# Main matmuls of a two-layer kernel as pairs of 64-row halves, low-rank part spread over the steps

## The chip, the cores and the metric

One core of one Trainium2 chip runs one launch. The metric is the device time in microseconds. TensorE multiplies, VectorE (DVE) and ScalarE (ACT) copy, subtract and activate, GpSimd (POOL) and SyncE (SP) mostly start transfers.

## The reference

The input x is 32 sequences of 64 tokens with 1024 features, in fp32. Two layers:

```
h  = cond(x): 64 x 64 matrix of the sequence's condition, over the tokens
x  = x + W3 (silu(W1 h + b1) * (W2 h + b2)) + b3           1024 x 1024 each
y  = W x + B[i] (A[i] x)            i: adapter of the sequence, rank 16
c  = softmax(keys . (Wq mean(y)) / sqrt(128))               8 experts
x  = x + W_org y + sum_e c_e up_e (down_e y)                rank 64 each
```

## The kernel before

Features lie on the partitions, tokens along the free dimension. The tokens are worked in two halves of 1024, each in six stages: `up0`, `up1` (the two halves of W1 and W2 with the gate), `down` (W3), `lin` (W with the adapters), `exp` (W_org and the experts' down matrix), `expup` (the experts' up matrix).

A stage other than `expup` computes its 2 x 2 block product with 7 block products instead of 8 (Strassen's scheme in the form with reused sums; the page calls them by i = 0 to 6). `S1` to `S4` are sums of input blocks, `T1` to `T4` sums of weight blocks, all made by VectorE (lines 927 to 938 and 979). `expup` has 4 plain products. The list `PRODUCTS` has 78 entries (stage, i).

A product has 4 groups of 128 output rows (`exp` has 6: the last two are the experts' down matrix), each group in its own PSUM bank of 512 columns. Every operand is split in a high and a low part of type fp32r: ScalarE casts `s_hi` and `t_hi` (lines 809, 828), VectorE subtracts for `s_lo` and `t_lo` (line 897). A group is 4 row blocks `p` of 128 times 3 terms: hi x hi (line 634), hi x lo (635), lo x hi (636), 12 matmuls of 128 rows, 128 output columns and 512 tokens. The main matmuls are 340 x 12 = 4080. `s` has two buffers, `t` has four slots of two groups (a half).

When a group is done it counts in `group_done`, and a half (two groups) is taken from its banks by one operation on 1024 columns: `snap` (ScalarE copy, line 840), `add` (VectorE, line 995), `addb` with bias (per group, line 1005), `gate` (per group, line 1027), `eadd` (line 1015) or `esnap` (line 843). Products i = 0, 2, 3, 4 use banks 0 to 3, the others banks 4 to 7, groups 4 and 5 of `exp` a table. `wait_bank_free` holds TensorE until the former content of a bank is taken.

Each engine's program runs in order, written out by hand in a loop over the products n. VectorE in loop n: the takings left from n - 1, `s_lo` of n + 1, `t_lo` of n + 1, gates, S sums, T sums, taking of half 0 of n. ScalarE: `s_hi` of n + 1, snaps left from n - 1, `t_hi` of n + 1, silus, first snap of n.

The low-rank part of `lin` (`lora_out`) is added in products 1, 4, 5 and 6: `xr` holds A x masked so that rows 0 to 63 serve tokens 0 to 255 and rows 64 to 127 the others. It runs as one lump after group 1: 4 turns of 2 fp32 matmuls of 64 rows and 256 columns (each two records in the profile), the two on different row halves of the array and different banks; turns 2 and 3 wait for turns 0 and 1 (`lora_crossed`), since two row halves may not write one bank at once. `route` puts the router's small matmuls (lines 743, 749, 757) after group 5 of `exp` 3 and group 1 of `exp` 4 and 5. `mixing` (line 731) makes the conditional product at the start of each half; `lora_in` (line 713) makes A x in `lin` 0 and 1.

Of the kernel before, what the change touches and what calls it, by code (L numbers as in the profile page):

```python
# [12 lines left out]
P = 128  # L13
# [4 lines left out]
TN = 512  # L18
# [82 lines left out]

def s_new(n):
    return S_LAST.index(S_LAST[S_ID[n]]) == S_ID[n] and not (kind_of(n) == "expup" and PRODUCTS[n][1] >= 2)


def t_halves(n, when):
# [100 lines left out]

GROUP_AT, SNAP_AT, SUM_AT, TMADE_AT, LOAD_AT = {}, {}, {}, {}, {}  # L210
for _n in range(LAST + 1):
    for _g in range(groups_in(_n)):
        GROUP_AT[_n, _g] = len(GROUP_AT) + 1
    _acts = (act_snaps(_n - 1) + act_silus(_n - 1) if _n else []) + act_first(_n)
    for _what in _acts:
        SNAP_AT[_what] = len(SNAP_AT) + 1
    _dves = (dve_after(_n - 1) + dve_post(_n - 1) if _n else []) + dve_own(_n)[0] + dve_own(_n)[1] + dve_scales(_n)
    for _what in _dves:
        SUM_AT[_what] = len(SUM_AT) + 1
    for _what in t_sums_beside(_n):  # L220
        TMADE_AT[_what] = len(TMADE_AT) + 1
# [23 lines left out]
def t_at(n, j):  # L245
    return T_ID[n, j] + 1
# [10 lines left out]
def build(nc, x_pairs, x_t, idx, cond_t, b_upgate, b_down, lora_a, lora_b, keys_t, wq_t,  # L257
# [3 lines left out]
    with ExitStack() as ctx:  # L261
# [62 lines left out]
        a_laid = sem("a_laid")  # L324
        b_diffed = sem("b_diffed")
        xr_full, xr_ready = sem("xr_full"), sem("xr_ready")
        lora_crossed = sem("lora_crossed")
        y_summed = sem("y_summed")
        q_full, q_copied = sem("q_full"), sem("q_copied")
        scores_full = sem("scores_full")  # L330
# [294 lines left out]
                    store(h, u, 1)  # L625

        def tensor_engine(pe):
            def product(n, g, p, start, stop):
                out = banks[:, bank_of(n, g), :]
                at, slot = (g % 2 * 4 + p) * P, T_ID[n, g // 2] % 4  # L630
                w_hi, w_lo = t_hi[:, slot, at:at + P], t_lo[:, slot, at:at + P]
                slot = S_ID[n] % 2
                x_hi, x_lo = s_hi[:, slot, p * TN:(p + 1) * TN], s_lo[:, slot, p * TN:(p + 1) * TN]
                pe.matmul(out, w_hi, x_hi, start=start, stop=False, skip_group_check=True)  # L634
                pe.matmul(out, w_hi, x_lo, start=False, stop=False, skip_group_check=True)  # L635
                return pe.matmul(out, w_lo, x_hi, start=False, stop=stop, skip_group_check=True)  # L636

            def wait_bank_free(n, g):

# [39 lines left out]
                else:  # L679
                    wait_taken(pe, n - {2: 2, 3: 1, 4: 1, 5: 4, 6: 1}[i], g)  # L680

            def lora_out(n):

                s, i = PRODUCTS[n]
                t = 1 if i >= 5 else 0
                crossed = 2 * (4 * STAGES[s][0] + (1, 4, 5, 6).index(i))
                for turn in range(4):
                    if turn >= 2:  # L690
                        pe.wait_ge(lora_crossed, crossed + turn - 1)
                    for j in range(2):
                        g, rows = 2 * (turn % 2) + (turn // 2 + j) % 2, slice(64 * j, 64 * (j + 1))
                        col = (g if i in (1, 6) else 4 + g) * P
                        last = pe.matmul(banks[:, bank_of(n, g), j * 2 * P:(j + 1) * 2 * P],  # L695
                                         lora_b_sb[rows, t, col:col + P], xr[rows, t, :],
                                         start=turn == 1 and i in (1, 5), stop=False, skip_group_check=True)
                    if turn < 2:
                        last.then_inc(lora_crossed, 1)
                    if turn == 2:  # L700
                        last.then_inc(group_done, 2)

            def lora_in(h, t, bank):
                s = stage_of(h, "lin")
# [26 lines left out]
                        last = pe.matmul(out[:, k, :], x_c[:, k * P:(k + 1) * P], mix[:, c, :], start=True, stop=True)  # L731
                    last.then_inc(mixed_full, 1)

            def route(n, g):

                s, i = PRODUCTS[n]
                h = STAGES[s][0]
                if (i, g) == (3, 5):
# [7 lines left out]
                if (i, g) == (4, 1):  # L746
# [4 lines left out]
                if (i, g) == (5, 1):  # L751
                    wait_taken(pe, n - 1, 3)
                    pe.wait_ge(rows_done, h + 1)
                    pe.wait_ge(consts_made, 5)
                    for k in range(KE):
                        rows = coef_rows[:, 2 * k:2 * k + 2, :].rearrange("b e r -> b (e r)")
                        last = pe.matmul(coef_bank[:, k * BH:(k + 1) * BH], rows, ident[:, :],
                                         start=True, stop=True)
                    last.then_inc(coef_full, 1)

            pe.wait_ge(mix_zeroed, 2)
            for n in range(LAST + 1):
                s, i = PRODUCTS[n]
# [6 lines left out]
                for g in range(groups_in(n)):  # L770
                    pe.wait_ge(s_ready, S_ID[n] + 1)
                    pe.wait_ge(t_ready, t_at(n, g // 2))
                    wait_bank_free(n, g)
                    fresh = g >= 4 or kind == "expup" or i in (0, 1, 5)
                    begun = lora and g >= 2
                    for p in range(4):
                        last = product(n, g, p, fresh and p == 0 and not begun, p == 3)
                    if lora and g == 1:
                        pe.wait_ge(xr_ready, h * TILES + (2 if i >= 5 else 1))
                        pe.wait_ge(b_gathered, (h + 1) * BH * 16)  # L780
                        if i == 6:
                            pe.wait_ge(b_diffed, h + 1)
                        wait_bank_free(n, 2)
                        wait_bank_free(n, 3)
                        lora_out(n)
                    elif not lora or g >= 2:
                        last.then_inc(group_done, 1)
                    if kind == "exp":
                        route(n, g)

        def scalar_engine(act):
            for j in range(2):
# [77 lines left out]
            for n in range(LAST + 1):  # L870
                s, i = PRODUCTS[n]
                h, kind = STAGES[s]
                if n < LAST and kind_of(n + 1) != "up0" or i < 6 and kind == "up0":
                    s_split(n + 1)
                if n > 0:
                    take(act_snaps(n - 1))
                if n < LAST:
                    t_split(n + 1, 0)
                if n > 0:
                    take(act_silus(n - 1))  # L880
                if kind == "down" and i in (2, 3):
                    lay_a(h, i - 2)
                take(act_first(n))
                if n < LAST:
                    t_split(n + 1, 1)
                if kind == "exp" and i == 4:
                    act.wait_ge(bias_done, h + 1)
                    act.activation(sexp[:, :], router[0:BH, 32:32 + E], ACT.Exp, bias=sbias[:, :],
                                   scale=SCORE_SCALE, accum_out=ssum[:, :]).then_inc(exp_done, 1)
                if n < LAST:  # L890
                    t_split(n + 1, 2)
                if kind == "expup" and i == 3 and h + 1 < HALVES:
                    mixing(h + 1)

        def vector_engine(dve):
# [186 lines left out]
            for n in range(LAST + 1):  # L1082
# [9 lines left out]
                    s_split(n + 1)  # L1092
                if n < LAST:
                    t_split(n + 1, 0)
                if kind == "lin" and i == 1:
                    mask_xr(h, 1, 7)
                if n > 0:
# [12 lines left out]
                if kind == "exp" and i == 4:  # L1110
                    largest(h)
                if kind == "exp" and i == 5:
                    copy_coef(h)
                if n < LAST:
                    t_split(n + 1, 1)
                if kind == "exp":
# [2 lines left out]
                take(dve_own(n)[1])  # L1119
                if kind == "exp" and i == 4:  # L1120
                    soften(h)
                take(dve_scales(n))
                if n < LAST:
                    t_split(n + 1, 2)
# [69 lines left out]
```

## Time and profile before

| | us |
|---|---|
| median of 3 runs | 1012.61 (1011.53 to 1012.75) |
| the profiled execution | 1012.33 |
| its span, first to last instruction | 1010.5 |
| TensorE busy | 990.6, 4772 matmul records |
| VectorE busy | 743.0 |
| ScalarE busy | 391.3 |
| mean granted TensorE clock | 0.998 |

PE is TensorE's matmuls, PEld its weight loads; the two overlap, and so do the records of successive matmuls. The distance from start to start tells what a matmul costs, its duration does not.

### The profile page before, as it was taken

To read this page: it belongs to the slowest core of one execution; us is meant where nothing else is said; L and a number is where in the kernel's file an instruction comes from. 1 tells how busy PE (TensorE), PEld (TensorE's weight loads), DVE (VectorE), ACT (ScalarE), POOL (GpSimd) and SP (SyncE) were. 2 spreads that over 40 slices of the span, in tenths; PEclk is the share of its full clock that TensorE was granted. 3 is DMA by queue.
4 is the path that set the end of the run, shared out by engine and by line. 5 is a ranking of instruction groups with operands and counts; after the bars stand their busy time and mean duration, and the time that the engine had idled before them with its cause. 6 is when DMAs were issued, how large, how long until landed. Compare 5 with 4: busy or idle time off the path is not lost.

```text
span 1010.5 us, 12337 instructions
## 1 busy us (share of the span) xinstructions
PE 990.6 (98%) x4772; PEld 820.0 (81%) x4772; DVE 743.0 (74%) x574; ACT 391.3 (39%) x349; POOL 33.8 (3%) x55
## 2 busy tenths in 40 slices
PE   6999999999999999999999999999999999999997
PEld 6888888878787888888888888888778878888886
DVE  2877977997866889674437888789885859877641
ACT  6563553543344333331055544543342532423110
POOL 1500000000000000000100000000000000000011
PEclk9999999999999999999999999999999999999999
DMA  8122044034013001322331211521330230021012
GB/s 279 76 84 104 1 157 175 23 112 159 1 42 131 36 1 63 149 100 89 121 126 42 83 42 40 210 84 32 121 140 2 75 134 0 1 105 42 1 63 104
DMA packets 22985, 84.68 MB, mean 84 GB/s; under 512 B 2690, under 2 KB 6802, under 8 KB 17042
## 3 DMA queue, kind: packets, MB, share of 16 engines
q1 hardware_dynamic: 20370, 74.98, 20.6%
q0 software_dynamic: 2400, 8.41, 2.2%
q8 instruction: 39, 0.64, 0.3%
q10 hardware_dynamic: 160, 0.52, 0.2%
q14 instruction: 16, 0.13, 0.0%
HBM read 75.51 MB, written 8.39 MB: 83 GB/s over the span
## 4 chain that ended last, share of the span: by engine, by line
PE 95%; DVE 2%; DMA 1%; issue 1%; ACT 0%; POOL 0%; POOLq 0%; ACTq 0%
PE banks L634 30%; PE banks L635 30%; PE banks L636 30%; PE banks L731 3%; PE banks L695 2%; PE banks L713 1%; DMA st<-x_pairs_in 1%; DMA cond_sb<-cond_t_in 1%; DVE st L938 0%; DVE w L979 0%; DVE s_lo L897 0%; ACT s_hi L809 0%; DVE r L995 0%; PE banks L743 0%; DVE t_lo L897 0%
## 5 line engine op out<-in xcount | busy, mean ns | idle before, releaser
L634 PE MATMUL banks<-s_hi,t_hi 128*128 128x512 f32 x1360 | 531.7, 391 | 2.8 <-DVE r L995 2.8
L635 PE MATMUL banks<-s_lo,t_hi 128*128 128x512 f32 x1360 | 529.4, 389 | 0.0
L636 PE MATMUL banks<-s_hi,t_lo 128*128 128x512 f32 x1360 | 529.2, 389 | 0.0
L634 PEld LDWEIGHTS banks<-s_hi,t_hi 128*128 128x128 f32 x1360 | 255.2, 188 | 60.0 <-issue 7.2
L636 PEld LDWEIGHTS banks<-s_hi,t_lo 128*128 128x128 f32 x1360 | 255.3, 188 | 53.3
L635 PEld LDWEIGHTS banks<-s_lo,t_hi 128*128 128x128 f32 x1360 | 255.3, 188 | 52.3
L995 DVE TENSOR_TENSOR r<-banks,r 128x1024 f32<-128x1024 f32 x92 | 111.4, 1221 | 100.3 <-PE banks L636 95.7
L897 DVE TENSOR_TENSOR t_lo<-w,t_hi 128x1024 fp32r<-128x1024 f32 x132 | 156.6, 1220 | 3.2 <-ACT t_hi L828 3.2
L809 ACT CAST s_hi<-st 128x2048 fp32r<-128x2048 f32 x40 | 76.5, 1912 | 197.7 <-PE banks L636 145.0
L828 ACT CAST t_hi<-w 128x1024 fp32r<-128x1024 f32 x132 | 133.3, 1048 | 50.4 <-PE banks L636 50.4
L809 ACT CAST s_hi<-r 128x2048 fp32r<-128x2048 f32 x34 | 65.0, 1913 | 206.7 <-PE banks L636 181.7
L897 DVE TENSOR_TENSOR s_lo<-st,s_hi 128x2048 fp32r<-128x2048 f32 x40 | 91.7, 2292 | 51.4 <-ACT s_hi L809 51.3
L897 DVE TENSOR_TENSOR s_lo<-r,s_hi 128x2048 fp32r<-128x2048 f32 x34 | 77.9, 2290 | 57.0 <-ACT s_hi L809 57.0
L979 DVE TENSOR_TENSOR w<-w 128x1024 f32<-128x1024 f32 x48 | 57.3, 1221 | 0.0
L828 ACT CAST t_hi<-we 128x1024 fp32r<-128x1024 f32 x30 | 30.9, 1052 | 60.0 <-PE banks L636 52.5
L840 ACT COPY r<-banks 128x1024 f32<-128x1024 f32 x40 | 40.4, 1010 | 24.4 <-PE banks L636 20.0
L731 PE MATMUL banks<-mix,st 128*128 128x128 f32 x256 | 32.3, 292 | 8.9 <-POOL mix L450 7.9
L731 PEld LDWEIGHTS banks<-mix,st 128*128 128x128 f32 x256 | 31.8, 207 | 9.2 <-issue 9.2
L1015 DVE TENSOR_TENSOR r<-banks,r 128x1024 f32<-128x1024 f32 x14 | 17.0, 1223 | 28.8 <-PE banks L636 28.8
L897 DVE TENSOR_TENSOR t_lo<-we,t_hi 128x1024 fp32r<-128x1024 f32 x30 | 36.0, 1221 | 0.0
L617 POOL DMA_DIRECT2D out_t<-r x16 | 11.6, 727 | 522.0 <-DVE r L995 522.0
L1005 DVE SCALAR_TENSOR_TENSOR r<-banks,b_dn_sb,r 128x512 f32<-128x512 f32 x32 | 22.3, 747 | 7.6 <-PE banks L636 7.6
(59 smaller groups left out, 329.9 us busy)
## 6 DMA issues: line engine op xcount, KB each, us to landing
w<-w_up_in SPq DMA_DIRECT2D x16, 1024.0 KB, 4.8
w<-w_base_in SPq DMA_DIRECT2D x10, 1024.0 KB, 4.8
st<-x_pairs_in SPq DMA_DIRECT2D x16, 512.0 KB, 5.7
w<-w_down_in SPq DMA_DIRECT2D x8, 1024.0 KB, 5.3
r<-x_t_in SPq DMA_DIRECT2D x8, 1024.0 KB, 6.2
w<-w_lin_in SPq DMA_DIRECT2D x8, 1024.0 KB, 5.2
out_t<-r POOLq DMA_DIRECT2D x16, 512.0 KB, 3.2
we<-w_expin_in SPq DMA_DIRECT2D x10, 512.0 KB, 4.5
```

The costliest lines, as they stand in the source:

```text
L634: pe.matmul(out, w_hi, x_hi, start=start, stop=False, skip_group_check=True)
L635: pe.matmul(out, w_hi, x_lo, start=False, stop=False, skip_group_check=True)
L636: return pe.matmul(out, w_lo, x_hi, start=False, stop=stop, skip_group_check=True)
L695: last = pe.matmul(banks[:, bank_of(n, g), j * 2 * P:(j + 1) * 2 * P], lora_b_sb[rows, t, col:col + P], xr[rows, t, :], start=turn == 1 an ...
L731: last = pe.matmul(out[:, k, :], x_c[:, k * P:(k + 1) * P], mix[:, c, :], start=True, stop=True)
L809: act.copy(s_hi[:, S_ID[n] % 2, :], s_source(n)).then_inc(s_hi_done, 1)
L828: act.copy(t_hi[:, T_ID[n, j] % 4, :], t_source(n, j)).then_inc(t_hi_done, 1)
L840: act.copy(half_block(n, at), half_banks(n, at)).then_inc(snapped, 1)
L897: return dve.tensor_tensor(out, value, hi.bitcast(F32), ALU.subtract)
L979: dve.tensor_tensor(out, left, right, ALU.subtract).then_inc(t_made, 1)
L995: dve.tensor_tensor(half_block(n, at), half_banks(n, at), half_block(n, at), ALU.add).then_inc(summed, 1)
L1005: dve.scalar_tensor_tensor(out=group_block(n, at), in0=banks[:, bank_of(n, at), :], scalar=b_dn_sb[:, m:m + 1], in1=group_block(n, at), op ...
```

## The change

Every product runs in steps (pair of groups, back). In a step with back = 0 each main matmul becomes two of 64 rows: rows 0 to 63 into the bank of the pair's first group, rows 64 to 127 into that of the second; with back = 1 the rows are exchanged. So a step is 4 x 3 x 2 = 24 matmuls. The order of steps is in `steps`. The second step of a pair waits for `crossed` of the first. Both groups are counted done together, at the end of the second step. The low-rank part is two matmuls at the end of each of the four steps. `route` follows other places: step (2, 1) of `exp` 3, (0, 0) of `exp` 4, (1, 1) of `exp` 5. On ScalarE the snaps left over go ahead of `s_hi`, and the exponential ahead of `t_hi` of the second half; on VectorE `largest` goes ahead and `copy_coef` behind. Both functions `half_rows` and `lora_half` replace `product` and `lora_out`.

```diff
+def steps(n):
+    if groups_in(n) == 4:
+        return [(0, 0), (1, 0), (0, 1), (1, 1)]
+    if PRODUCTS[n][1] == 1:
+        return [(0, 0), (1, 0), (0, 1), (1, 1), (2, 0), (2, 1)]
+    return [(0, 0), (1, 0), (0, 1), (2, 0), (1, 1), (2, 1)]
...
-            def product(n, g, p, start, stop):
-                out = banks[:, bank_of(n, g), :]
-                at, slot = (g % 2 * 4 + p) * P, T_ID[n, g // 2] % 4
-                w_hi, w_lo = t_hi[:, slot, at:at + P], t_lo[:, slot, at:at + P]
-                slot = S_ID[n] % 2
-                x_hi, x_lo = s_hi[:, slot, p * TN:(p + 1) * TN], s_lo[:, slot, p * TN:(p + 1) * TN]
-                pe.matmul(out, w_hi, x_hi, start=start, stop=False, skip_group_check=True)
-                pe.matmul(out, w_hi, x_lo, start=False, stop=False, skip_group_check=True)
-                return pe.matmul(out, w_lo, x_hi, start=False, stop=stop, skip_group_check=True)
+            def half_rows(n, g, p, j, term, start):
+                rows, at = slice(64 * j, 64 * (j + 1)), (g % 2 * 4 + p) * P
+                weights = (t_hi, t_hi, t_lo)[term][rows, T_ID[n, g // 2] % 4, at:at + P]
+                acts = (s_hi, s_lo, s_hi)[term][rows, S_ID[n] % 2, p * TN:(p + 1) * TN]
+                return pe.matmul(banks[:, bank_of(n, g), :], weights, acts, start=start, stop=False,
+                                 skip_group_check=True)
...
+            def lora_half(n, g, j):
+                i, rows = PRODUCTS[n][1], slice(64 * j, 64 * (j + 1))
                 t = 1 if i >= 5 else 0
...
+                col = (g if i in (1, 6) else 4 + g) * P
+                return pe.matmul(banks[:, bank_of(n, g), j * 2 * P:(j + 1) * 2 * P], lora_b_sb[rows, t, col:col + P],
+                                 xr[rows, t, :], start=False, stop=False, skip_group_check=True)
...
+                for pair, back in steps(n):
+                    if back:
+                        pe.wait_ge(crossed, CROSSED_AT[n, pair])
+                    else:
+                        pe.wait_ge(s_ready, S_ID[n] + 1)
+                        pe.wait_ge(t_ready, t_at(n, pair))
+                        for g in groups_of(pair):
+                            wait_bank_free(n, g)
                     for p in range(4):
-                        last = product(n, g, p, fresh and p == 0 and not begun, p == 3)
-                    if lora and g == 1:
+                        for term in range(3):
+                            for j in range(2):
+                                last = half_rows(n, 2 * pair + (back + j) % 2, p, j, term, (fresh or pair == 2)
+                                                 and not back and p == 0 and term == 0)
+                    if lora:
                         pe.wait_ge(xr_ready, h * TILES + (2 if i >= 5 else 1))
...
+                        for j in range(2):
+                            last = lora_half(n, 2 * pair + (back + j) % 2, j)
+                    if back:
+                        last.then_inc(group_done, 2)
+                    else:
+                        last.then_inc(crossed, 1)
                     if kind == "exp":
-                        route(n, g)
+                        route(n, pair, back)
...
@@ scalar_engine
+                if n > 0:
+                    take(act_snaps(n - 1))
                 if n < LAST and kind_of(n + 1) != "up0" or i < 6 and kind == "up0":
                     s_split(n + 1)
-                if n > 0:
-                    take(act_snaps(n - 1))
```

## Rows read from the trace of the kernel before

**Rows 1.** The page: busy time by engine, granted clock by slice, chain that ended last.

```profile
PE 990.6 (98%) x4772; PEld 820.0 (81%) x4772; DVE 743.0 (74%) x574; ACT 391.3 (39%) x349; POOL 33.8 (3%) x55
...
PEclk9999999999999999999999999999999999999999
...
PE banks L634 30%; PE banks L635 30%; PE banks L636 30%; PE banks L731 3%; PE banks L695 2%; PE banks L713 1%; DMA st<-x_pairs_in 1%; DMA cond_sb<-cond_t_in 1%; DVE st L938 0%; DVE w L979 0%; DVE s_lo L897 0%; ACT s_hi L809 0%; DVE r L995 0%; PE banks L743 0%; DVE t_lo L897 0%
```

**Rows 2.** Groups by shape: count, busy us, mean ns, idle before.

```profile
L634 PE MATMUL banks<-s_hi,t_hi 128*128 128x512 f32 x1360 | 531.7, 391 | 2.8 <-DVE r L995 2.8
...
L634 PEld LDWEIGHTS banks<-s_hi,t_hi 128*128 128x128 f32 x1360 | 255.2, 188 | 60.0 <-issue 7.2
...
L695 PEld LDWEIGHTS banks<-xr,r 64*128 64x128 f32 x128 | 11.6, 185 | 4.0 <-issue 2.8
```

**Rows 3.** Busy time in stretches (length; PE, PEld, DVE, ACT, POOL): up1, down, lin.

```profile
101.35:177.50 76.15, 76.15 (x337) 63.06 (x336) 62.27 (x48) 37.26 (x35) 0.00 (x0) 1.00 0.29 111
177.50:255.40 77.90, 76.48 (x337) 62.80 (x335) 69.85 (x58) 31.03 (x27) 1.29 (x1) 1.00 0.28 95
258.76:345.93 87.17, 87.17 (x468) 70.28 (x465) 61.61 (x42) 32.21 (x28) 0.00 (x0) 1.00 0.17 61
```

**Rows 4.** Timeline (start us, duration us, engine) around the first low-rank lump.

```profile
277.09 0.39 PE L636 MATMUL banks<-s_hi,t_lo 128*128 128x512 f32 x1
277.41 1.60 PEld L695 LDWEIGHTS banks<-xr,r 64*128 64x128 f32 x16 [0.35 <-issue]
277.41 2.00 PE L695 MATMUL banks<-xr,r 64*128 64x256 f32 x16
...
279.34 0.50 PE L634 MATMUL banks<-s_hi,t_hi 128*128 128x512 f32 x1
...
279.68 0.40 PE L635 MATMUL banks<-s_lo,t_hi 128*128 128x512 f32 x1
...
279.92 0.40 PE L636 MATMUL banks<-s_hi,t_lo 128*128 128x512 f32 x1
```

**Rows 5.** TensorE of line 695 in short stretches (x: records touched by the stretch).

```profile
277.72:277.94 0.22, 0.22 (x4) 1.00 0.00 0
...
278.38:278.59 0.21, 0.21 (x4) 1.00 0.00 0
```

**Rows 6.** Full-row fp32: mixing in one stretch, then the router's matmuls in the timeline.

```profile
18.00:25.05 7.05, 7.05 (x65) 7.05 (x64) 1.00 0.93 309
...
411.21 1.85 PE L743 MATMUL banks<-y_sum,cond_sb 128*128 128x16 f32 x16
412.92 0.49 PE L634 MATMUL banks<-s_hi,t_hi 128*128 128x512 f32 x1
```

**Rows 7.** Timeline of VectorE in down, products 2 and 3.

```profile
208.37 1.22 DVE L995 TENSOR_TENSOR r<-banks,r 128x1024 f32<-128x1024 f32 x1
210.35 1.23 DVE L995 TENSOR_TENSOR r<-banks,r 128x1024 f32<-128x1024 f32 x1 [0.76 <-PE banks L636]
212.30 2.29 DVE L897 TENSOR_TENSOR s_lo<-st,s_hi 128x2048 fp32r<-128x2048 f32 x1 [0.72 <-ACT s_hi L809]
214.51 2.35 DVE L897 TENSOR_TENSOR t_lo<-w,t_hi 128x1024 fp32r<-128x1024 f32 x2
216.78 2.29 DVE L938 TENSOR_TENSOR st<-r 128x2048 f32<-128x2048 f32 x1
218.98 2.35 DVE L979 TENSOR_TENSOR w<-w 128x1024 f32<-128x1024 f32 x2
221.25 2.35 DVE L995 TENSOR_TENSOR r<-banks,r 128x1024 f32<-128x1024 f32 x2
```

**Rows 8.** Waits of TensorE: us in total, times, longest.

```profile
PE banks L634 <- DVE r L995: 2.8, 2, 1.4
```

**Rows 9.** Timeline at the end of down: VectorE, then TensorE.

```profile
256.03 2.72 DVE L1005 SCALAR_TENSOR_TENSOR r<-banks,b_dn_sb,r 128x512 f32<-128x512 f32 x4
...
256.88 1.95 PE L713 MATMUL banks<-r 128*32 128x128 f32 x64 [1.33 <-issue]
```

More of the change, by code:

```diff
@@ L206, in dve_scales @@
     return [("scale", n, 0), ("scale", n, 1)] if kind_of(n) == "exp" and PRODUCTS[n][1] == 5 else []
-GROUP_AT, SNAP_AT, SUM_AT, TMADE_AT, LOAD_AT = {}, {}, {}, {}, {}
+GROUP_AT, CROSSED_AT, SNAP_AT, SUM_AT, TMADE_AT, LOAD_AT = {}, {}, {}, {}, {}, {}
 for _n in range(LAST + 1):
+    for _pair, _back in steps(_n):
+        if not _back:
+            CROSSED_AT[_n, _pair] = len(CROSSED_AT) + 1
     for _g in range(groups_in(_n)):
@@ L326, in build @@
         xr_full, xr_ready = sem("xr_full"), sem("xr_ready")
-        lora_crossed = sem("lora_crossed")
+        crossed = sem("crossed")
         y_summed = sem("y_summed")
@@ L680, in wait_bank_free @@
                     wait_taken(pe, n - {2: 2, 3: 1, 4: 1, 5: 4, 6: 1}[i], g)
-            def lora_out(n):
-                s, i = PRODUCTS[n]
+            def lora_half(n, g, j):
+                i, rows = PRODUCTS[n][1], slice(64 * j, 64 * (j + 1))
                 t = 1 if i >= 5 else 0
[L688 to L701, printed above, removed]
+                col = (g if i in (1, 6) else 4 + g) * P
+                return pe.matmul(banks[:, bank_of(n, g), j * 2 * P:(j + 1) * 2 * P], lora_b_sb[rows, t, col:col + P],
+                                 xr[rows, t, :], start=False, stop=False, skip_group_check=True)
             def lora_in(h, t, bank):
@@ L732, in mixing, with route @@
                     last.then_inc(mixed_full, 1)
-            def route(n, g):
+            def route(n, pair, back):
                 s, i = PRODUCTS[n]
                 h = STAGES[s][0]
-                if (i, g) == (3, 5):
+                if (i, pair, back) == (3, 2, 1):
                     pe.wait_ge(wq_loaded, 16)
@@ L745, in route @@
                     last.then_inc(q_full, 1)
-                if (i, g) == (4, 1):
+                if (i, pair, back) == (4, 0, 0):
                     pe.wait_ge(q_copied, h + 1)
@@ L750, in route @@
                               start=True, stop=True).then_inc(scores_full, 1)
-                if (i, g) == (5, 1):
+                if (i, pair, back) == (5, 1, 1):
                     wait_taken(pe, n - 1, 3)
@@ L769, in tensor_engine @@
                 lora = kind == "lin" and i in (1, 4, 5, 6)
[L770 to L775, printed above, removed]
-                    for p in range(4):
-                        last = product(n, g, p, fresh and p == 0 and not begun, p == 3)
-                    if lora and g == 1:
+                fresh = kind == "expup" or i in (0, 1, 5)
+                for pair, back in steps(n):
[6 more added lines that the diff above has]
+                            wait_bank_free(n, g)
+                    for p in range(4):
+                        for term in range(3):
[3 more added lines that the diff above has]
+                    if lora:
                         pe.wait_ge(xr_ready, h * TILES + (2 if i >= 5 else 1))
@@ L782, in tensor_engine @@
                             pe.wait_ge(b_diffed, h + 1)
[L783 to L787, printed above, removed]
+                        for j in range(2):
[4 more added lines that the diff above has]
+                        last.then_inc(crossed, 1)
                     if kind == "exp":
-                        route(n, g)
+                        route(n, pair, back)
         def scalar_engine(act):
@@ L883, in scalar_engine @@
                 take(act_first(n))
-                if n < LAST:
-                    t_split(n + 1, 1)
                 if kind == "exp" and i == 4:
@@ L889, in scalar_engine @@
                                    scale=SCORE_SCALE, accum_out=ssum[:, :]).then_inc(exp_done, 1)
+                if n < LAST:
+                    t_split(n + 1, 1)
                 if n < LAST:
@@ L1094, in vector_engine @@
                     t_split(n + 1, 0)
+                if kind == "exp" and i == 4:
+                    largest(h)
                 if kind == "lin" and i == 1:
@@ L1109, in vector_engine @@
                 take(dve_own(n)[0])
[L1110 to L1113, printed above, removed]
                 if n < LAST:
@@ L1121, in vector_engine @@
                     soften(h)
+                if kind == "exp" and i == 5:
+                    copy_coef(h)
                 take(dve_scales(n))
```

## The prediction, made before any run of the changed kernel

> **What bounds the kernel now.** I read the page first. TensorE is busy for 990.6 of 1010.5 us, its clock is granted in full in nearly every slice, and nine tenths of the chain that ended last lie on the three lines of the main matmul [rows 1]. So what counts is how far apart two main matmuls start, and where TensorE waits. The grouped instructions give the number of them: 3 x 1360 = 4080, each with its own weight load of 188 ns that lies beside a stream [rows 2]. The table by stretches then gives their distance: in one stage without any wait, 7 products of 48 matmuls take 76.15 us, so 0.2266 us each; the next stage takes 77.90 us up to its last product's end, 1.6 us more [rows 3]. A stream of 512 columns at the granted 2.4 GHz lasts 512/2.4 = 213.3 ns. Each matmul therefore carries 13.3 ns in which nothing streams: 4080 x 13.3 = 54 us in the whole kernel. That gap is the only large thing that this change can touch, because it takes no column out.
>
> **What a pair costs (the term that decides).** After the change a step is 12 pairs: two 512-column streams side by side, on rows 0-63 and 64-127, on two banks, each with its own 128-column weight load. A product of four groups is 4 steps, so 48 pairs, in the place of 48 matmuls. The trace of before has no pair of this kind. Its nearest row is the low-rank part at line 695: 16 records in 2.00 us, 64 x 256, in full fp32 [rows 4]. Cut into windows of 0.21 to 0.22 us, every window touches four of them, two that began in it and two that end in it [rows 5]. So two do run side by side, and the next two follow 0.216 us later. A record there is 256 columns at two cycles, as long a stream as the main one (213.3 ns), and the gap is 2.7 ns instead of 13.3. If the main pairs behave so, one costs 0.2160, and the gain is 4080 x (0.2267 - 0.2160) = 43.7 us.
>
> The row does not prove it. It differs from the main matmul in two things: 64 rows instead of 128, and fp32 at two cycles a column instead of one. The mixing matmuls are full-row fp32: 65 records within 7.05 us, of which two or three began before the window, so about 0.112 us for 128 columns x 2 cycles = 0.107 us [rows 6]. Full rows alone do not bring a gap of 13 ns, then; that speaks for the data rate or for the weight load read beside a full-rate stream as its cause, which halving the rows need not cure. So the bounds are: 0.2160 at best (line 695), 0.2267 if the gap stays, and 2 x 13.3 ns on 213.3 = 0.2400 if the gap is a price for each load. I take 0.2160, since line 695 is nearest in rows, in load and in length of stream, but only at a little over one half.
>
> The Trainium skill ("TensorE: Matmul & The Clock Gate", section "Wait — 56ns, not 53.3ns?") has 215.7 ns between back-to-back matmuls of 512 columns, that is 2.5 ns over the stream. The trace disagrees for the present form (226.6) and agrees for the line 695 pairs (216); by that figure the sum would be the one above.
>
> **The low-rank part.** Now it is four turns of two matmuls in one lump. From the last full matmul before it, 277.09, to the second one behind it, 279.68, lie 2.59 us where two distances would be 0.45; then a few distances of 0.24 follow before the old rhythm returns [rows 4]: 2.19 us in all. Of these 8 x 0.216 = 1.73 is streaming, some 0.20 lies on either side where the engine goes from 128 to 64 rows and back, and 0.06 is the slow rhythm. Spread over the four steps, the streaming stays and the changes of form go: 8 x 0.46 = 3.7 us gained.
>
> **New changes of form.** The router's matmuls of 128 rows stand now between full-row matmuls: 16 records from 411.21 in 1.85 us, and the next main one starts at 412.92, as soon as their loads allow [rows 6]. After the change both sides are a change of form, 0.2 each by rows 4. With mixing to first product the same. The column-form and 16-row matmuls (lines 713, 749, 757) pay it already. Bounds: 0 and 6 x 0.4 = 2.4 us; I take 1.5.
>
> **The new waits.** Each second step waits for `crossed` of the first step of the same pair of banks. In 76 of 78 products another step of 2.59 us lies between, and inside line 695 the same kind of wait costs nothing (the 0.216 goes on through it). In product 1 of each `exp` stage steps (2,0) and (2,1) are adjacent: the end of the last matmul (0.39 us after its start), the signal and the way in cost about 0.4, twice: 0.8 us. Behind this wait stands everything on TensorE, and nobody else.
>
> **What comes later or is needed earlier.** Groups 0 and 1 are now finished after 3/4 of a product instead of 1/4 and 1/2; t of the second half and the second pair of banks are needed after 1/4 instead of 1/2. So the cover for taking a bank out shrinks from 5.4 to 2.6 us (products 3, 4 and 6 reuse the banks of the product before). The cost of taking is 1.23 us on VectorE or 1.0 on ScalarE; what matters is the queue ahead. On ScalarE the snaps now go ahead of the 1.9 us s_hi; on VectorE the `largest` of the router goes earlier, because its result is now needed at step 4 of `exp` 4; both fit by about 2 us. Where VectorE has room (`up1` and `lin`: 62.27 of 76.15 and 61.61 of 87.17 us [rows 3]; `up0` and `expup` are like `up1` or emptier) the add of the first half starts at 3/4 + 0.2 us and ends 1.2 us before the next product. There I lose about 0.3 us per half, at product 2 of the `up` stages, whose t_lo would be ready 0.1 to 0.2 late.
>
> `down` is the place where VectorE is full: 69.85 of 77.90 us [rows 3], one operation on another, with two gaps of 0.7 us around 210 only [rows 7]. Worked with those durations (add 1.14 apart, s_lo 2.20, t_lo 1.14, S 2.20, T 1.14), with the start of `down` 0 as zero: add(down 2, half 0) ends at 32.6, about where product 3 begins now (3 x 10.88 = 32.64), but TensorE would be there at 31.4. Product 3 then starts at the old time and three products gain nothing. The wait ahead of product 4 (1.4 us of TensorE, twice [rows 8]) is for add(3, half 0), behind S3 and two T sums [rows 7]. Its queue starts 1 us sooner, because the product before no longer ends last: product 4 gains 1.1, products 5 and 6 0.5 each together with it. At the end of the stage TensorE already waits 1.3 us for the bias add behind four T sums, which hangs on the same s_hi [rows 9]; there nothing is gained. `down` gives 2.3 of 3.6 us a half: 1.3 x 2 = 2.6 lost, and 0.6 for the `up` stages. For waits that I have not found, 0 to 8, I take 2.
>
> **The instruction stream.** 4080 more matmuls and loads. In the low-rank lump 32 records pass in 2.00 us, 62 ns each with the streams as their bound; a main pair has 4 in 216 ns, 54 each. Loads and DMA bytes of data are unchanged. Cost nought while TensorE's queue is full.
>
> **Sum.** The profiled execution took 1012.33 us around a span of 1010.5; the median of three is 1012.61, 0.03% above. 1012.33 - 43.7 - 3.7 + 1.5 + 0.8 + 2.6 + 0.6 + 2 = 972.4 us.
>
> **The rivals.**
> - *The gap stays* (0.2267 a pair). For it: the full-row fp32 rows without a gap [rows 6], which leave the full-rate stream as the cause. Then only the low-rank gain remains, -3.7 + 1.5 + 0.8, and since products are no shorter the `down` queue is as now, with 0 to 2 of new waits: 1011 to 1014, say 1012.
> - *The two loads are served one after the other.* The 128-row loads of line 743 follow each other every 0.112 us (16 in 1.71 us, with 16-column streams [rows 6]); two would be 0.223, more than the stream. Gain 4080 x 0.0034 = 13.9: about 998. Against it: at line 695 all 16 loads and 16 streams pass at 0.216 a pair, though loads there could also hide by luck. The Trainium skill (the same page, "LDWEIGHTS (loading the stationary operand)") says that load time goes by columns and not by rows, so halving the rows would double the load work; that speaks against the change, and a 64-row load lasts 185 ns and a 128-row load 188 [rows 2], so the trace agrees on one load and leaves open whether two go side by side at the full rate.
> - *Slower: the gap is paid once for each load.* Two tiles each load while both stream, so a pair is 213.3 + 2 x 13.3 = 0.240: 4080 x 0.0133 = 54 us more, about 1066. It decides from a pair of 0.2270 upwards. Against it: at line 695 the pair has less gap than the single matmul.
> - *The pairs don't run side by side at full rate.* 0.43 a pair, some 1880 us. Line 695 runs them at half the data rate only, so it is not excluded; nearly.
>
> **How the numbers follow.** Chances: pairs at 0.216 0.52 (own range 963 to 990, with waits from 0 to 8 and a pair from 0.2150 to 0.2190); loads in turn 0.07; gap stays 0.22, of which within 0.2% 0.17, faster 0.02, slower 0.03; gap per load 0.14; anything worse 0.05. About 0.2% (2 us) is what a measurement of this kernel can tell. Faster 0.52 + 0.07 + 0.02 = 0.61, same 0.17, slower 0.14 + 0.03 + 0.05 = 0.22. The range reaches from the low end of the first case over the second and third: 962 to 1016, which holds 0.81.
>
> **What would show it.** Main matmuls in twos a few ns apart, the next two 0.216 later; `up1` in about 72.7 us instead of 76.15; plain products of 10.4 and `exp` products of 15.6 us; low-rank products about 12.1; a wait for VectorE's line 995 ahead of product 3 of `down` too. A pair at 0.227 or 0.240 makes the prediction wrong whatever else holds; a pair at 0.216 with more than 8 us of new TensorE waits says that the cover of the banks was the misjudged part.

## The result and the profile after

| | before | after |
|---|---|---|
| median, us | 1012.68 (4 runs, 1011.53 to 1013.48) | 1024.65 (4 runs, 1023.01 to 1027.08) |
| ratio to before | | 1.0121 (95%: 1.0097 to 1.0145) |
| profiled execution, us | 1012.33 | 1023.86 |

The changed kernel is slower by 12 us. The forecast was 972.4, so the direction was wrong, and the time lies outside the range of 962 to 1016.

The page of the kernel after, with the lines that answer to [rows 1, 2], and the instruction queue (packets, MB; before it had 39 and 0.64):

```profile
PE 994.1 (97%) x8852; PEld 857.7 (84%) x8852; DVE 744.0 (73%) x574; ACT 392.4 (38%) x349; POOL 33.9 (3%) x55
...
q8 instruction: 71, 1.16, 0.5%
...
L646 PE MATMUL banks<-s_hi,t_hi 64*128 64x512 f32 x2720 | 552.1, 393 | 8.3 <-DVE xr L1048 5.3
...
L646 PEld LDWEIGHTS banks<-s_hi,t_hi 64*128 64x128 f32 x2720 | 268.8, 185 | 54.5 <-issue 10.8
```

Every main matmul has become two (2720 for 1360 on one of three terms), as the diff says, and before them stands a releaser that was not there: VectorE's mask of the low-rank part, 5.3 us. The stretches that answer to [rows 3], `up1`, `down` and `lin` of the first half:

```profile
103.56:179.72 76.16, 76.16 (x676) 62.94 (x673) 62.27 (x48) 37.48 (x35) 0.00 (x0) 1.00 0.30 111
179.72:257.60 77.88, 76.34 (x674) 68.35 (x672) 69.78 (x58) 31.04 (x27) 1.29 (x1) 1.00 0.28 96
261.34:351.63 90.29, 87.62 (x802) 83.46 (x800) 61.16 (x42) 32.21 (x28) 0.00 (x0) 0.98 0.17 59
```

Read the first line against 76.15 us before: 7 x 48 = 336 pairs take 76.16 us, 0.2267 each, to four digits what one full-row matmul cost. `down` is as before too (77.88 against 77.90). `lin` took 87.17 in the stretch of [rows 3] and takes 90.29 here. The timeline of TensorE in `up0` (start, duration, x: records) shows the pairs, two records together and the next two 0.22 to 0.23 us later:

```profile
60.03 0.39 PE L646 MATMUL banks<-s_hi,t_lo 64*128 64x512 f32 x2
60.26 0.39 PE L646 MATMUL banks<-s_hi,t_hi 64*128 64x512 f32 x2
60.49 0.39 PE L646 MATMUL banks<-s_lo,t_hi 64*128 64x512 f32 x2
```

The halves do run side by side at the full rate, then; what did not come is the shorter gap. And in `lin` product 1 stands the only large wait that was not there before (the first line; the second is the wait of [rows 8]):

```profile
PE banks L646 <- DVE xr L1048: 5.3, 2, 2.7
PE banks L646 <- DVE r L1001: 2.8, 2, 1.5
```

```profile
275.40 2.29 DVE L903 TENSOR_TENSOR s_lo<-st,s_hi 128x2048 fp32r<-128x2048 f32 x1 [4.38 <-ACT s_hi L815]
...
277.18 0.59 PE L699 MATMUL banks<-xr,r 64*128 64x256 f32 x4
277.62 2.35 DVE L903 TENSOR_TENSOR t_lo<-we,t_hi 128x1024 fp32r<-128x1024 f32 x2
279.88 0.42 DVE L1048 TENSOR_TENSOR xr<-banks,half_mask 128x256 f32<-128x256 f32 x1
...
280.45 0.50 PE L646 MATMUL banks<-s_hi,t_hi 64*128 64x512 f32 x2 [2.67 <-DVE xr L1048]
...
281.22 0.69 PE L646 MATMUL banks<-s_hi,t_hi 64*128 64x512 f32 x2
...
281.64 0.69 PE L646 MATMUL banks<-s_lo,t_hi 64*128 64x512 f32 x2
...
282.07 0.69 PE L646 MATMUL banks<-s_hi,t_lo 64*128 64x512 f32 x2
```

The first fence is TensorE's waits (us in total, times, longest), the second the timeline. The second low-rank input lies in bank 7 until VectorE masks it out (`mask_xr`, line 1048), and group 3 of `lin` 1 writes to bank 7. Before, group 3 began at three quarters of the product. Now the pair of groups 2 and 3 is the second step and begins at one quarter. VectorE still makes `s_lo` and two `t_lo` first, so TensorE stands for 2.67 us. A little behind the wait the pairs start 0.42 to 0.43 us apart instead of 0.227. The granted clock (the last three columns are the clock, DMA share and GB/s), below for the idle time and two stretches behind it,

```profile
277.40:280.40 3.00, 0.38 (x4) 0.00 (x0) 2.90 (x4) 0.00 (x0) 0.00 (x0) 1.00 0.00 0
280.40:281.21 0.81, 0.76 (x6) 0.76 (x8) 0.00 (x0) 0.00 (x0) 0.00 (x0) 1.00 0.00 0
281.21:284.62 3.41, 3.41 (x18) 3.14 (x16) 0.00 (x0) 0.00 (x0) 0.00 (x0) 0.50 0.00 0
```

is still full for 0.8 us when the matmuls go on, then half, the level of 1.2 GHz, for 3.41 us. The eight pairs or so at that level cost 8 x 0.2 = 1.6 us more. So `lin` 1 lasts 17.17 us, start to start, against 13.20 before, in both halves.

### The profile page after: what moved, and what is told of

It is laid out like the page before. It is cut to its first block, busy times and chain, and to the rows that moved or that the text cites. A ratio compares the mean times of both kernels' runs of the same rounds, so it can differ in the third digit from the quotient of the medians.

```text
span 1022.1 us, 20505 instructions
## 1 busy us (share of the span) xinstructions
PE 994.1 (97%) x8852; PEld 857.7 (84%) x8852; DVE 744.0 (73%) x574; ACT 392.4 (38%) x349; POOL 33.9 (3%) x55
## 3 DMA queue, kind: packets, MB, share of 16 engines
q8 instruction: 71, 1.16, 0.5%
## 4 chain that ended last, share of the span: by engine, by line
PE 93%; DVE 3%; DMA 2%; issue 1%; ACT 1%; POOL 0%; POOLq 0%; ACTq 0%; DVEq 0%
PE banks L646 88%; PE banks L730 2%; DMA st<-x_pairs_in 1%; PE banks L699 1%; DVE t_lo L903 1%; DVE s_lo L903 1%; ACT s_hi L815 1%; DMA cond_sb<-cond_t_in 1%; DVE w L985 0%; PE banks L712 0%; PE banks L742 0%; DVE st L944 0%; DVE r L1001 0%; PE banks L756 0%; POOLq L1134 0%
## 5 line engine op out<-in xcount | busy, mean ns | idle before, releaser
L646 PE MATMUL banks<-s_hi,t_hi 64*128 64x512 f32 x2720 | 552.1, 393 | 8.3 <-DVE xr L1048 5.3
L646 PE MATMUL banks<-s_hi,t_lo 64*128 64x512 f32 x2720 | 545.0, 387 | 0.0
L646 PE MATMUL banks<-s_lo,t_hi 64*128 64x512 f32 x2720 | 544.8, 387 | 0.0
L646 PEld LDWEIGHTS banks<-s_hi,t_hi 64*128 64x128 f32 x2720 | 268.8, 185 | 54.5 <-issue 10.8
L646 PEld LDWEIGHTS banks<-s_hi,t_lo 64*128 64x128 f32 x2720 | 268.9, 185 | 42.6
L646 PEld LDWEIGHTS banks<-s_lo,t_hi 64*128 64x128 f32 x2720 | 269.4, 185 | 41.9
L1001 DVE TENSOR_TENSOR r<-banks,r 128x1024 f32<-128x1024 f32 x92 | 111.4, 1221 | 124.4 <-PE banks L646 99.7
L834 ACT CAST t_hi<-w 128x1024 fp32r<-128x1024 f32 x132 | 133.3, 1048 | 83.6 <-PE banks L646 83.5
L846 ACT COPY r<-banks 128x1024 f32<-128x1024 f32 x40 | 40.7, 1017 | 105.8 <-PE banks L646 91.7
L864 ACT COPY r<-banks 128x1024 f32<-128x1024 f32 x16 | 15.8, 1014 | 30.3 <-PE banks L730 30.3
```

Of the source, the lines that this page charges most:

```text
L646: return pe.matmul(banks[:, bank_of(n, g), :], weights, acts, start=start, stop=False, skip_group_check=True)
L834: act.copy(t_hi[:, T_ID[n, j] % 4, :], t_source(n, j)).then_inc(t_hi_done, 1)
L846: act.copy(half_block(n, at), half_banks(n, at)).then_inc(snapped, 1)
L864: act.copy(dst[:, :, c % 4 * P:(c % 4 + 1) * P], src).then_inc(mixed_copied, 1)
L1001: dve.tensor_tensor(half_block(n, at), half_banks(n, at), half_block(n, at), ALU.add).then_inc(summed, 1)
```

## The experiments

Theory after the first reading: the gap of 13.3 ns belongs to the data type fp32r and not to the rows (so halving them brings nothing), and the loss is the mask's place in VectorE's queue. Rivals: the gap comes from loading 128 weight rows or columns beside the stream; the loss comes from the halves themselves or from the order of steps.

**A series of forms alone.** The kernel m1 computes nothing of the reference; it runs 24 or 48 matmuls of each form one behind the other.

```diff
+            for i in range(N):
+                pe.matmul(banks[:, 1, :], w_r[:, i % 4 * P:(i % 4 + 1) * P], x_r[:, :], start=i == 0, stop=False, skip_group_check=True)
...
+            for i in range(N):
+                pe.matmul(banks[:, 3, :], w_b[:, i % 4 * P:(i % 4 + 1) * P], x_b[:, :], start=i == 0, stop=False, skip_group_check=True)
```

These are line 42 (fp32r) and line 60 (bf16). Line 44 takes 64 of the 128 weight columns, line 50 256 of the 512 tokens, line 52 rows 0 to 63 alone, line 56 fp32 operands with 256 tokens.

> A program of its own with nothing of the reference computed: 13 series of 24 to 48 matmuls without any wait, one form a series, to measure the distance from start to start. The changed kernel shows 0.2267 us a pair of 64-row main matmuls, as the 128-row matmul before, so rows are not what brings the 13.3 ns over the stream of 213.3. Three theories of what does. Rate (a fixed price of each matmul that streams fp32r at a column a cycle): 0.2267 for 128, 64 and 32 weight columns, 0.173 for 384 columns streamed; bf16 streams at the same rate, so 0.2267 too if the rate alone counts, 0.216 if the bytes do. Load (the 128-column weight load is read beside a full-rate stream): 64 weight columns 0.220, 32 weight columns 0.2167, 384 streamed 0.173. Length (a share of the columns streamed): 384 streamed 0.170, weight columns without effect. All three: full fp32 with 256 columns at two cycles 0.216 for 128 rows as for pairs of 64; one 64-row half alone 0.2267.

Per series (min, median and max duration in ns, then first and last start in us):

```profile
L42 PE MATMUL banks<-x_r,w_r x24: 388/389/389, 21.8 to 27.0; 128*128 128x512 f32 x24
L44 PE MATMUL banks<-x_r,w_r x24: 387/390/398, 27.3 to 32.5; 128*64 128x512 f32 x24
L50 PE MATMUL banks<-x_r,w_r x24: 278/283/283, 42.5 to 45.3; 128*128 128x256 f32 x24
L52 PE MATMUL banks<-x_r,w_r x24: 386/386/497, 45.5 to 50.8; 64*128 64x512 f32 x24
L56 PE MATMUL banks<-raw x48: 379/379/483, 56.6 to 66.8; 128*128 128x256 f32 x48
L60 PE MATMUL banks<-x_b,w_b x24: 379/379/389, 77.7 to 82.7; 128*128 128x512 bf16 x24
```

The number to take is (last start - first start) / (count - 1): 5.2 / 23 = 0.226 for L42, 5.0 / 23 = 0.217 for bf16, 10.2 / 47 = 0.217 for fp32. The single records give it to the nanosecond, at the steady rhythm:

| form | start to start, ns | stream at 2.4 GHz | gap |
|---|---|---|---|
| fp32r 128 rows, 128 weight columns, 512 | 226.7 | 213.3 | 13.4 |
| the same, 384 columns | 173.4 | 160.0 | 13.4 |
| the same, 256 columns | 120.0 | 106.7 | 13.3 |
| fp32r, 64 or 32 weight columns, 512 | 230.0, 231.7 | 213.3 | 17, 18 |
| fp32r, 64 rows | 226.6 | 213.3 | 13.3 |
| fp32, 256 columns of two cycles, 128 rows or pairs | 215.8 | 213.3 | 2.5 |
| bf16, 512 columns, 128 rows or pairs | 215.8 | 213.3 | 2.5 |

The gap goes with fp32r alone. It doesn't depend on the length of the stream, on the rows, nor on the weight load, which falls from 188 ns (128 columns) to 134 (64) and 109 (32) while the gap grows. This table settles which forms have it; why fp32r has it, no run shows. The form of the changed kernel itself, 24 pairs of fp32r halves (line 54), is not in the table because it has no single rhythm there: one row half goes at 0.2267 us throughout, the other, which starts earlier, at 0.226 to 0.240. Neither goes at 0.216.

**The mask first.** On the kernel after, in VectorE's loop:

```diff
+                if kind == "lin" and i == 1:
+                    mask_xr(h, 1, 7)
                 s_split(n + 1)
...
-                if kind == "lin" and i == 1:
-                    mask_xr(h, 1, 7)
```

> The changed kernel with one edit: in lin 1 VectorE makes the mask of xr (which empties bank 7) ahead of the s_lo and t_lo of the next product. In the changed kernel TensorE waits 2.9 us in each half for this mask at step (1, 0) of lin 1 and then runs some 8 pairs at the lower clock, 1.7 us. If that wait is what the loss hangs on: 2 x 4.6 us gone, about 1015.4. If something else of the order is late there as well (the ScalarE snap ahead of s_hi), under 2 us of it goes: about 1022.

1013.6 us (12 runs), ratio to before 1.0009 (0.9999 to 1.0018): the same as before. `lin` of the first half lasts

```profile
260.60:346.46 85.86, 85.86 (x804) 70.56 (x802) 61.30 (x42) 32.21 (x28) 0.00 (x0) 1.00 0.17 62
```

4.4 us less than the 90.29 of after and without idle time; `lin` 1 lasts 12.70. Over two halves that is 8.9 us, and with 0.7 at the start (first product at 26.74 us instead of 27.47) it is nearly the whole difference of the two profiled executions, 9.7. The medians lie 11.0 apart; the other 1.4 us no trace explains.

**The order of steps with full rows.** The kernel after, all its waits and its order kept, but each step works one group with 128 rows (12 matmuls instead of 24).

```diff
-                            for j in range(2):
-                                last = half_rows(n, 2 * pair + (back + j) % 2, p, j, term, ...)
+                            last = full_rows(n, 2 * pair + back, p, term, ...)
```

> The changed kernel with the order of steps, waits, counts and low-rank passes kept, but each step is 12 matmuls of full 128 rows on one group instead of 24 halves on two. If halving the rows is neutral (0.2267 either way) and the order makes the whole loss, the products without low-rank part keep their times to 0.1 us; the low-rank passes are now each between two changes of form, 0.4 us x 4 x 8 = 12.8 us, less the slow rhythm saved: about 1036. If the halves cost something of their own (twice the instructions and loads), products get shorter than 10.88 and the time lies under 1030.

1030.1 us, ratio 1.0182 (1.0166 to 1.0198). First `up1`, then `lin`:

```profile
100.13:176.29 76.16, 76.16 (x338) 63.06 (x336) 62.27 (x48) 37.48 (x35) 0.00 (x0) 1.00 0.30 111
257.66:353.96 96.30, 93.83 (x468) 69.36 (x464) 62.06 (x42) 32.21 (x28) 0.00 (x0) 0.98 0.16 55
```

`up1` is 76.16 with halves and with full rows, so the halves are neutral where nothing else differs. The wait for the mask is there too (4.9 us, twice, longest 2.5): it belongs to the order, not to the halves. The low-rank products last 14.37 us against 12.80 of after: each of the four low-rank parts now lies between 128-row matmuls, and (14.37 - 12.80) / 4 = 0.39 us is what a change of form there and back costs, close to the 0.4 that I had put in. Still I had expected 1036. What I left out lies elsewhere: against after, `lin` takes 10.4 us more over both halves, but the first product starts at 23.85 us instead of 27.47, and the last product of the first half with the mixing behind it takes 25.73 instead of 27.13. The clock differs too. The wait for the mask is 2.47 us in each half; in the first, 3.41 us at a granted clock of 0.50 follow and `lin` 1 takes 18.42 us, in the second the clock stays full and it takes 16.87:

```profile
764.28:859.02 94.74, 92.27 (x468) 68.23 (x464) 62.05 (x42) 32.21 (x28) 0.00 (x0) 1.00 0.15 56
```

So the half clock is worth 1.55 us here, and it does not follow each time.

**The back step at once.** Halves, but the exchanged step follows directly on its first one, so that each pair of banks waits for a matmul that has only just been issued.

```diff
+    return [(pair, back) for pair in range(groups_in(n) // 2) for back in (0, 1)]
```

> The changed kernel with another order of steps: each pair's second step right behind its first, so (0,0), (0,1), (1,0), (1,1) and so on. It tests what the exchange one step later is for. In the changed kernel the two adjacent steps of exp 1 show a distance of 0.44 instead of 0.227 us between two matmuls, 0.215 for one such wait. Now there are 2 of them in each of 64 products and 3 in each of 14, 170 in all instead of 2: 168 x 0.215 = 36 us more. But pair 1 begins after 1/2 of a product, as before the change, so the wait of 2.9 us for the mask of xr and its 1.7 us at the lower clock go: 1024.65 + 36 - 9 = about 1051. If a wait right behind costs the full 0.4 us that the prediction gave it, 1083.

1072.6 us, ratio 1.0597 (1.0575 to 1.0618). `up1`:

```profile
108.20:189.60 81.40, 80.53 (x676) 61.88 (x673) 62.39 (x49) 37.34 (x35) 0.00 (x0) 1.00 0.29 104
```

81.40 - 76.16 = 5.24 us for 14 adjacent waits, 0.375 each; a product is 11.63 instead of 10.88. The prediction's 0.4 for such a wait holds. Over the whole kernel the 168 waits more cost 59.0 us against the kernel with the mask first, 0.35 each, since some of them fall into time that `down` waits anyway. The 0.215 on which the smaller of my expectations rested was read off one distance beside the wait and was wrong.

**Taking the banks first in `down`.** On the kernel before, VectorE takes half 0 ahead of the T sums in products 3 and 6; a second kernel has this and the mask first on the kernel after.

```diff
+                taken_first = kind == "down" and i in (3, 6)
+                if taken_first:
+                    take(dve_own(n)[0])
...
```

> The kernel before with one edit: in products 3 and 6 of down VectorE takes the first half from its banks ahead of the T sums and not behind them. If TensorE's waits at these two places are for that take alone, 1.45 us goes ahead of product 4 and 1.3 us ahead of lora_in, in each half: 5.5 us, 1007.1. If VectorE is the bound of the stage, the T sums come 1.2 to 2.4 us later and what needs them or the next s_lo waits instead: no change, 1012.6.

1006.2 us, ratio 0.994 (0.9928 to 0.9953): `down` 3 falls from 12.46 to 10.88 us, `down` 6 with the `lora_in` behind it from 14.26 to 12.86, and the waits of [rows 8] and the 1.33 us of [rows 9] are gone. The part of the prediction that located these waits in VectorE's queue holds.

> The changed kernel with the mask first and the first half of down 3 and 6 taken ahead of the T sums. With full rows the second edit alone took away 1.58 us ahead of down 4 and 1.40 at the end of down. Here the half is ready 2.7 us later (after 3/4 of the product instead of 1/2), so VectorE gets to it before it is ready in down 6 and waits some 1.7 us with the T sums behind it: 1.5 us gained at down 3, between 0 and 1.4 at down 6, in each half: 1007.8 to 1010.6 from the 1013.6 of the run with the mask first. If VectorE is late with what follows, no gain: 1013.6.

1007.4 us, ratio 0.996 (0.9944 to 0.9977), with the same two products at 10.88 and 12.91. So with these waits mended the halves stand at 1007.4 and the full rows at 1006.2, and the intervals overlap.

**The other data type.** To see whether the rest of the sum holds at the pace that it assumed, the high and low parts become bf16, on the kernel before (c1) and on e1 (c2). Nothing of the computation is left out, but both parts of the split keep fewer bits.

```diff
-        s_hi, s_lo = sb("s_hi", [P, 2, 4 * TN], F32R), sb("s_lo", [P, 2, 4 * TN], F32R)
-        t_hi, t_lo = sb("t_hi", [P, 4, 8 * P], F32R), sb("t_lo", [P, 4, 8 * P], F32R)
+        s_hi, s_lo = sb("s_hi", [P, 2, 4 * TN], BF16), sb("s_lo", [P, 2, 4 * TN], BF16)
+        t_hi, t_lo = sb("t_hi", [P, 4, 8 * P], BF16), sb("t_lo", [P, 4, 8 * P], BF16)
```

> The kernel before with one edit: the high and low parts s_hi, s_lo, t_hi, t_lo are bf16 instead of fp32r (the same three products of 128 rows, 512 columns, coarser low parts). The series of one form a line showed 0.2158 us a bf16 matmul of 128 rows and 0.2267 an fp32r one, whatever its rows and weight columns. If the 13.3 ns is the data type's, products go from 10.88 to 10.36: 4080 x 0.0109 = 44.5 us less, of which the stage down gives back 1.3 a half because VectorE sets its pace: about 971. If the gap has another cause in this kernel (banks read by VectorE beside, waits), under half of that.

> The changed kernel with the mask of xr made first (as in the run with that edit alone) and all high and low parts bf16 instead of fp32r. Now a pair of halves costs the 0.216 us that was forecast for fp32r, so this tests the other steps of that sum (the order, the waits for crossed, down, the low-rank passes) at the pace they were worked out for: it gave 972.4. If the shorter cover of the banks costs more than was found, 980 and above, with waits for VectorE or ScalarE in the rows of TensorE. Against the same data type with full rows (about 971) it shows what halves and order are worth without the gap: nothing, plus or minus 2 us.

c1 967.8 us, ratio 0.9565 (0.9549 to 0.9581); c2 969.6, 0.9585 (0.9564 to 0.9606). `up1` of c1 and of c2, then `down` of c2 (171.16 to 248.50):

```profile
97.17:169.73 72.56, 72.19 (x330) 32.82 (x336) 62.09 (x48) 37.12 (x35) 0.00 (x0) 1.00 0.31 116
```

```profile
98.58:171.16 72.58, 72.58 (x675) 38.21 (x672) 62.16 (x48) 37.36 (x35) 0.00 (x0) 1.00 0.32 117
171.16:248.50 77.34, 73.44 (x676) 38.00 (x672) 71.83 (x61) 32.78 (x28) 1.27 (x1) 1.00 0.29 96
```

c2's wait of TensorE for the banks in `down` (us in total, times, longest):

```profile
PE banks L647 <- DVE r L1002: 3.7, 4, 1.2
```

Both run at 72.57 / 336 = 0.2160 a matmul or pair, halves or not. What the prediction expected of the halves is the data type's. The wait for the banks comes four times instead of twice, as foretold for product 3. It does so in c1 as well (3.6, 4, 1.1), so it comes with the shorter products and not with the halves.

**Both together.** The earlier takings with bf16, full rows (c3, on b1) and halves (c4, on a2).

> The kernel before with both edits that helped alone: bf16 parts, and the first half of down 3 and 6 taken ahead of the T sums. With bf16 alone down 3 lasts 11.21 instead of 10.36 us and down 6 with lora_in 14.46; with the take first the second should be 12.3 and the first 10.4: 3 us a half, 967.8 - 6 = 962. If VectorE is by now the bound of the whole stage (down 1 and 2 already last 10.9 to 11.6), the time only moves to the products behind: 965 to 968.

> The changed kernel with mask first, take first and bf16 parts, beside the same without the halves. The halves' gain is the low-rank part, 12.09 against 12.39 us a product, 2.4 us in all; against it stand 0.4 us at the router's first matmuls and 0.24 at exp 1 in each half, 1.2. If nothing else is late: 1 us faster than the full rows, about 961. If the first half, which is ready after 3/4 of a product, comes too late for VectorE in down 6, or the longer program costs something at the start and at the mixing: 963 to 965.

c3 964.1 us, 0.9525 (0.9512 to 0.9538); c4 963.5, 0.9518 (0.9505 to 0.9531). Their intervals overlap: the halves are worth nothing that can be measured here either. With full rows the low-rank part of `lin` 1 waits for the mask (0.7 us in each half; `lin` 1 takes 13.13 us, the other low-rank products of c3 12.39 and those of c4 12.1), which an earlier mask would probably mend; no run tries it. Both beat the kernel before by some 49 us, for fewer bits in the parts; b1 beats it by 6 us with the same arithmetic.

## Why the prediction was wrong, by its own steps

| step | forecast, us | measured, us |
|---|---|---|
| a pair at 0.2160 | -43.7 | 0.2267: 0 |
| low-rank spread over steps | -3.7 | 13.07 to 12.80, 8 times: -2.2 |
| router's changes of form | +1.5 | `exp` 3 18.02 to 18.30, `exp` 4 and 5 the same: +0.6 |
| adjacent steps of `exp` 1 | +0.8 | 16.32 to 16.75 and 16.73: +0.8 |
| `down` and `up` at the shorter pair | +3.2 | no shorter pair; `down` 81.25 to 81.40: +0.3 |
| waits not found | +2 | the mask: +9 |
| instruction stream (its cause open) | 0 | start +2.4, mixing +0.6: +3.0 |
| sum | -39.9 | +11.5 (profiled: +11.5) |

**The pair.** The step that failed is the sentence that chose 0.2160 because line 695 was nearest in rows, in load and in length of stream. It was not nearest in what counted. The prediction had named the difference itself (fp32 at two cycles a column) and had, with the mixing of [rows 6], a full-row row without the gap. Two forms stood without the gap, one with 64 rows and one with 128, and one with it. Rows had been varied by the trace already, in fp32, and had made no difference; what set the main matmul apart from both was fp32r, its column a cycle and its longer count of columns. A pair measured 0.2267 us, and the term of -43.7 us was 0. The rival "the gap stays" had the outcome and gave 1011 to 1014; the kernel with the mask mended measures 1013.6. Its cause, a stream at the full rate, was not right either: bf16 streams at the same rate with 2.5 ns (m1). That this lies within is partly luck, for 2.4 us of it are a later start and a longer mixing that the rival did not have. It deserved the larger chance. The Trainium skill's 2.5 ns between matmuls ("TensorE: Matmul & The Clock Gate", section "Wait — 56ns, not 53.3ns?") is met by bf16 and fp32 in m1 (215.8 against 213.3) and not by fp32r (226.7).

**The mask.** The part "needed earlier" said that t of the second half and the second pair of banks are needed after a quarter of the product. I applied it to `s`, `t` and the four banks' takings, and not to `mask_xr`, which also frees a bank. It is one of the 0 to 8 us of waits not found, so its kind was allowed for; its size is 2 x 2.67 us of idle time, 2 x 1.6 from the clock and some 0.2 in each half where the matmuls set in again: 9.

**The low-rank part.** The mechanism held, the size was off: 0.27 a product instead of 0.46. Behind the lump some ten matmuls went at a slower rhythm (distances of 0.224 to 0.240 instead of 0.227, 0.06 us in all); the same pattern stands behind each of the four passes, 0.05 each. In the bf16 kernels with halves the low-rank product is 12.09, as the prediction wrote (12.1); with full rows it is 12.39 there, so the spreading itself gives 0.30.

**The router.** 0.28 us at `exp` 3 and nothing at 4 and 5, and the same in bf16 (17.24 us in c3, 17.52 in c4). One change of form there and back was put at 0.4 and each half has three such places; only one of them costs anything.

**The instruction stream.** Costed at nothing on TensorE's queue, and there it costs nothing: the pairs keep 0.2267. But the first product starts at 27.47 us instead of 25.08, and the last product of the first half with the mixing behind it takes 27.13 instead of 26.50. Over all runs full-row kernels start the first product at 23.8 to 25.7 us (five, mean 24.6), kernels with halves at 25.3 to 27.5 (six, mean 26.4). Without that last product the mixing takes 14.7 to 15.6 us in the first and 15.9 to 17.2 in the second. The order of steps is not the cause: e2 has it with full rows and starts at 23.85. In the same runs x lands 5.2 to 5.7 us (median of 16 transfers) after its issue with full rows and 6.0 to 6.6 with halves, and the instruction queue moves 1.16 MB instead of 0.64. That the longer program's fetches hold up those loads fits, but no run varies the length of the program alone, so the cause stays open.

**What held.** At the pace that it assumed the rest of the sum can be tried as a whole: c2 has the change, the mask mended and 0.2160 a pair, and takes 969.6 us against the forecast of 972.4. `down` 3 starts 32.9 us after `down` 0, 33.2 in the second half (forecast 32.6), the stage gains 2.2 and 1.8 us (forecast 2.3), and product 2 of the `up` stages is late by 0.05 (forecast 0.1 to 0.2). That the sum comes so close is partly luck: start and mixing cost 2.7 us that it did not have, against 2 held for waits that are not there and 0.9 too much for the router. The other two rivals, loads in turn and the gap once per load, fall with 0.2267.

## What to carry to other kernels

When a gap per instruction is to be cut, list the rows with it and without it and look for the one property that separates them before trusting the row that looks most alike; here a run of 24 matmuls per form would have told it. When an order of steps changes, list every operation that frees a bank or a buffer, also the odd ones outside the regular takings, and set its place in its queue against the new time of need. And try the queue of the engine that frees the banks first: moving one addition ahead of two sums gave 6 us, while rebuilding every matmul gave nothing.

## What the runs showed of the hardware that was not expected

- At the full clock an fp32r matmul carries 13.3 ns beside its stream, for 256, 384 and 512 columns alike, with 64 or 128 rows; fp32 and bf16 carry 2.5. At the granted 0.50 the pairs of the kernel after start 0.42 to 0.43 us apart, which is the stream of 512 columns at 1.2 GHz (0.4267): there the gap isn't seen.
- Two loads of 64 rows for two row halves go side by side beside full-rate streams: two loads of 185 ns in every 226.7. Narrower weights don't speed up fp32r matmuls, they slow them (230.0 and 231.7 with 64 and 32 columns).
- A bf16 weight load takes 94 to 98 ns, an fp32r or fp32 one of the same size 184 to 191.
- A change between 128-row and 64-row matmuls and back costs 0.39 us (e2 against after, four in a product); a wait for the matmul just issued 0.375 (e3).
- 2.67 us of idle time in `lin` 1 were followed by 0.8 us at the full clock and then 3.41 us at 0.50, in both halves of the kernel after. 2.47 us of idle time in e2 were followed by 3.41 us at 0.50 in the first half and by none in the second, 1.55 us of time apart.
